# A recurrent chain of RNN, LSTM and mixture of experts: the RNN begins on the first 16 steps of x, and the LSTM follows 8 steps behind it

## The reference

```
x = x + rnn(x, cond)     # h = tanh(h @ Wh + x_t @ Wx + b), 256 steps, h0 = cond
x = x + lstm(x, cond)    # i, f, o, g from x_t @ Wx + b + h @ Wh; c = f*c + i*g; h = o*tanh(c)
x = x + moe(x, cond)     # shared expert gelu(x@sw1+sb1)@sw2+sb2, plus the 2 best of 4 experts,
                         # chosen per batch row from means of x over time
x = x + adapter(x, cond) # low-rank weights made from cond: gelu(x @ (down + a2 b2)) @ (up + a1 b1)
```

## Time and profile before

| | us |
|---|---|
| median of 3 runs | 1098.54 (1098.54 to 1099.82) |
| the profiled execution | 1100.26, its span 1098.3 |
| first RNN tanh | 19.06 |
| first LSTM gate activation (block 0 begins) | 39.60 |
| block 0 | 41.73 |
| block 8 (with low-rank rows), block 10 (plain) | 40.19, 38.68 |
| block 15 begins | 638.08 |

### The profile page before, as it was taken

The page is one execution under the profiler, slowest core; times in us unless marked ns, Lnnn a source line. Parts: engine busy times, 40 slices in busy tenths (PEclk is TensorE's granted clock), DMA queues, the critical chain, the costliest instruction groups (busy, mean ns, idle before and its releaser), DMA issues. The chain is left out here.

```text
span 1098.3 us, 56330 instructions
## 1 busy us (share of the span) xinstructions
PE 1068.6 (97%) x22334; PEld 979.2 (89%) x22334; DVE 825.8 (75%) x3566; ACT 649.0 (59%) x2495; POOL 287.0 (26%) x864
## 2 busy tenths in 40 slices
PE   6899999999999999999999999899999999999998
PEld 5789999899999999999999987788888888888887
DVE  6677878778877878887887786876666666676797
ACT  4567777677777777777777755333333333343476
POOL 3533333333333333333333310560000000000041
PEclk8759999999999999999999998999999999999999
DMA  8401211211211200000000011100000000000022
GB/s 262 104 23 57 62 28 57 62 43 42 61 50 36 64 22 19 19 19 19 19 9 5 4 33 14 17 1 2 2 1 2 2 2 2 2 4 2 3 92 82
DMA packets 54921, 37.01 MB, mean 34 GB/s; under 512 B 25560, under 2 KB 53514, under 8 KB 54668
## 3 DMA queue, kind: packets, MB, share of 16 engines
q1 hardware_dynamic: 54060, 33.12, 10.8%
q10 hardware_dynamic: 608, 0.30, 0.1%
HBM read 28.42 MB, written 4.98 MB: 30 GB/s over the span
## 5 line engine op out<-in xcount | busy, mean ns | idle before, releaser
L657 ACT ACTIVATE gel<-bank,seq 128x256 f32<-128x256 f32 x256 | 121.5, 475 | 215.2 <-PE bank L1298 211.3
L1296 PE MATMUL bank<-XHL,WE 128*128 128x256 f16 x768 | 210.3, 274 | 1.9 <-DVE XHL L883 1.3
L1296 PE MATMUL bank<-GH,WE 128*128 128x256 f16 x768 | 209.4, 273 | 2.5 <-DVE GH L910 1.8
L1298 PE MATMUL bank<-XHL,WE 128*128 128x256 f16 x768 | 210.7, 274 | 0.0
L1297 PE MATMUL bank<-XHL,WE 128*128 128x256 f16 x768 | 210.6, 274 | 0.0
L1298 PE MATMUL bank<-GH,WE 128*128 128x256 f16 x768 | 209.5, 273 | 0.0
L1297 PE MATMUL bank<-GH,WE 128*128 128x256 f16 x768 | 209.5, 273 | 0.0
L448 POOL TENSOR_TENSOR RH<-rf,RH 128x32 f16<-128x32 f32 x256 | 75.6, 295 | 395.4 <-ACT RH L597 395.3
L1296 PE MATMUL bank<-seq 128*128 128x64 f16 (+2 forms) x1216 | 165.4, 203 | 1.9 <-DVE oz L945 1.4
L1298 PE MATMUL bank<-seq 128*128 128x64 f16 (+2 forms) x1216 | 165.8, 204 | 0.0
L1297 PE MATMUL bank<-seq 128*128 128x64 f16 (+2 forms) x1216 | 165.8, 204 | 0.0
(11 more groups left out here) (218 smaller groups left out, 3362.6 us busy)
## 6 DMA issues: line engine op xcount, KB each, us to landing
stage<-in_L_cond_ew SPq DMA_DIRECT2D x64, 128.0 KB, 2.4
stage<-in_L_cond_W SPq DMA_DIRECT2D x32, 256.0 KB, 3.7
XHL<-in_x SPq DMA_DIRECT2D x8, 512.0 KB, 9.1
out<-WE SPq DMA_DIRECT2D x16, 256.0 KB, 2.2
stage<-in_L_cond_sw SPq DMA_DIRECT2D x2, 1024.0 KB, 5.4
scratch<-rows SPq DMA_DIRECT2D x96, 8.0 KB, 1.9
stage<-in_L_cond_Wx SPq DMA_DIRECT2D x1, 1024.0 KB, 9.2
stage<-in_L_cond_Wh SPq DMA_DIRECT2D x1, 1024.0 KB, 11.4
```

What stands on the lines that cost most here:

```text
L657: nc.scalar.activation(gel[:, m % 2, :], banks[m % len(banks)][:, 0:256], ACT.Gelu_apprx_tanh, scale=scale, bias=bias).then_inc(s["a_g"], 1)
L1296: MM(out_, w(HI), x(HI), start=start, stop=False, skip_group_check=True)
L1298: return MM(out_, w(HI), x(LO), start=False, stop=stop, skip_group_check=True)
```

## The change

1. **First x.** The first 16 times of all batches are loaded by 16 DMAs of 16 KB, 8 on SyncE's queue and 8 on ScalarE's ahead of its other loads; eight transposes in two banks turn them, ScalarE and VectorE copy one tile each. The RNN starts on that. The rest of x (8 DMAs of 512 KB) is loaded after the LSTM's weights, into a part of WE that the experts' weights fill later.
2. **Lag.** The LSTM runs LAG = 8 steps behind the RNN: 8 RNN steps alone in place of 16, with two LSTM weight pieces after each. TensorE has two x tiles after each of the lone steps 5, 6 and 7 and two before block 0. Block 15 gets 8 RNN steps.
3. **Turning the rest of x.** All 16 tiles are turned in block 0, in two banks (5 and 6) in place of four. TensorE turns tiles 0 and 1 ahead of LSTM step 0, tiles 2u+2 and 2u+3 at the end of steps u = 0, 1, 2, and tiles 8 to 15 one by one at the ends of steps 7 to 14. A tile waits for the copy of the tile two before it. ScalarE copies the even ones, VectorE the odd ones, at the ends of the steps in `X_OUT`.
4. **Tables.** New `HALVES`, `HALVES_LOW`, `X_TILES`, `EXPERT`, `EXPERT_LOW`, `SHARED_PIECES` (steps 3 to 15 in place of 0 to 14); the next block's x parts are made in steps 4 to 7 of the block before it; GpSimd splits x at other steps of a group; one seed moves by a step; two pieces of the gate's work in block 15 move by one or two steps.

```diff
-PAIR_FROM = 1
+LAG = 8
-        x_bank = [bank[0:4], [*bank[5:8], bank[1]]]
+        x_bank, cond_bank = bank[5:7], bank[7]
...
+        def load_first(engine, batches):
+            for b in batches:
+                engine.dma_start(xin_first[U * (b % G):U * (b % G) + U, b // G, :], a["x"][b, 0:U, :]
+                                 ).then_inc(s["ld_xf"], 16)
...
             # SyncE
-                for quarter in range(4):
-                    load_x(0, quarter)
+                load_first(sp, range(G))
                 ... RNN weights, biases, LSTM weights
-                for quarter in range(4):
-                    load_x(1, quarter)
+                for half in range(2):
+                    for quarter in range(4):
+                        load_x(half, quarter)
...
             # ScalarE
             act.sem_inc(s["a_g"], M)
+                load_first(act, range(G, B))
...
+            def x_out(k):
+                act.wait_ge(s["pe_x"], k + 1)
+                dst, src = x_tile(k)
+                nc.scalar.activation(dst, src, ACT.Copy).then_inc(s["a_x"], 1)
...
-            for r in range(U):
-                rnn_step(0, r)
+            for n in range(LAG):
+                rnn_step(n)
+                for _ in range(LSTM_PIECES[n]):
...
-                    if not last:
-                        rnn_step(it + 1, u)
+                    if it * U + u + LAG < T:
+                        rnn_step(it * U + u + LAG)
...
+                    for k in X_OUT[u] if first else ():
+                        if k % 2 == 0:
+                            x_out(k)
...
             # TensorE
+            def transpose_x(k):
+                half, i = divmod(k, 8)
                 if i % C == 0:
                     pe.wait_ge(s[f"ld_x{half * 4 + i // C}"], 16)
+                if k < 2:
+                    pe.wait_ge(s["v_xf" if k % 2 else "a_xf"], 1)
+                else:
+                    pe.wait_ge(s["v_x" if k % 2 else "a_x"], k // 2)
+                for j in range(4):
+                    last = nc.tensor.transpose(x_bank[k % 2][:, j * P:(j + 1) * P],
+                                               xin[:, half, 4 * (i // C) + j, (i % C) * P:(i % C + 1) * P], idf[:])
                 last.then_inc(s["pe_x"], 1)
...
+            for n in range(LAG):
+                rnn_step(n)
+                if n == LAG - 3:
+                    pe.wait_ge(s["v_wlo"], N_RNN + N_LSTM // 2)
+                    pe.wait_ge(s["v_const"], 6)
+                    ig_x(0, 0)
+                    ig_x(0, 1)
+                elif n == LAG - 2:
+                    ig_x(0, 2)
+                    ig_x(0, 3)
+                elif n == LAG - 1:
+                    f_x(0, 0, 0)
+                    f_x(0, 1, 0)
             for i in range(C):
                 o_x(0, i, 0)
+            for k in X_OUT[0]:
+                transpose_x(k)
             pe.wait_ge(s["v_wlo"], LSTM_SPLIT)
-            pe.wait_ge(s["v_x"], 12)
...
                     next_x(it * U + u)
+                    if first and u + 1 < U:
+                        for k in X_OUT[u + 1]:
+                            transpose_x(k)
...
-HALVES = [0, 2, 3, 2, 2, 3, 2, 2, 0, 2, 3, 2, 2, 3, 2, 2]
-HALVES_LOW = [0, 2, 3, 2, 3, 3, 2, 3, 0, 2, 3, 2, 1, 1, 2, 3]
+HALVES = [0, 3, 2, 1, 3, 2, 2, 3, 0, 3, 2, 1, 3, 2, 2, 3]
+HALVES_LOW = [0, 3, 2, 1, 3, 2, 2, 3, 1, 3, 3, 1, 2, 1, 2, 3]
-LSTM_PIECES = [0, 0, 2, 2] + [1] * 12
-X_HI, X_LO = (10, 14), (11, 15)
+LSTM_PIECES = [2] * LAG
+X_HI, X_LO = (4, 6), (5, 7)
+X_OUT = [(2 * u, 2 * u + 1) if u < 4 else (u,) if u >= 8 else () for u in range(U)]
-X_TILES = [[("f", 0)], [("f", 1), ("o", 0), ("o", 1)], [("ig", 0)], [("ig", 1), ("ig", 2), ("ig", 3)],
-           [("f", 0), ("f", 1)], [("o", 0)], [("o", 1), ("ig", 0), ("ig", 1)], [("ig", 2), ("ig", 3)]]
-EXPERT, EXPERT_LOW = (1, 5, 8, 13), (1, 6, 9, 12, 14)
+X_TILES = [[], [], [("f", 0), ("f", 1), ("o", 0)], [("ig", 0), ("ig", 1), ("ig", 2), ("ig", 3), ("o", 1)],
+           [], [("ig", 0), ("o", 0), ("o", 1)], [("f", 0), ("f", 1), ("ig", 1)], [("ig", 2), ("ig", 3)]]
+EXPERT, EXPERT_LOW = (1, 11, 13, 15), (1, 9, 12, 14, 15)
-SHARED_PIECES = [(u,) for u in range(U - 2)] + [(U - 2, U - 1), ()]
+SHARED_PIECES = [(), (), (), (0,), (1,), (2, 3), (4,), (5,), (6,), (7,), (8, 9), (10,), (11, 12), (13,), (14,), (15,)]
```

More of the change, by code:

```diff
@@ L450, in rnn_step @@
                 nc.gpsimd.tensor_tensor(x, x, rf[:, slot], ALU.add).then_inc(s["p_x1"], 1)
[L451 to L460, removed]
+                if n % H == H - 1:
+                    split_x1(n // H, HI)
+                if n >= H and n % H == 0:
+                    split_x1(n // H - 1, LO)
             def split_x1(k, part_):
@@ L488, in _ @@
             nc.gpsimd.memset(gate_bias[:, NIG + C:NIG + 2 * C], 0.0).then_inc(s["p_gate_bias"], 1)
[L489 to L493, removed]
+            for n in range(LAG, T):
+                rnn_step(n)
+            split_x1(T // H - 1, LO)
             pool.wait_ge(s["v_oh"], 1)
@@ L1061, in block_steps @@
                 for u in range(U):
-                    lstm_step(it, u, not last)
+                    lstm_step(it, u, it * U + u + LAG < T)
                     if last and u in extras:
                         extras[u]()
-                    x_at = X_LO_LOW if low_block(it) else X_LO
-                    if it < NB - 2 and u in x_at:
-                        x_lo(it + 2, x_at.index(u))
+                    if it < NB - 1 and u in X_LO:
+                        x_lo(it + 1, X_LO.index(u))
+                    for k in X_OUT[u] if first else ():
+                        if k % 2:
+                            x_out(k)
                     if u in QUARTERS:
@@ L1330, in _ @@
             for c in range(C):
-                last = nc.tensor.transpose(bank[4][:, (C + c) * B:(C + c + 1) * B], ln[:, c * P:(c + 1) * P],
+                last = nc.tensor.transpose(cond_bank[:, (C + c) * B:(C + c + 1) * B], ln[:, c * P:(c + 1) * P],
                                            idf[0:B, 0:B])
@@ L1337, in _ @@
                 for c in range(C):
-                    last = MM(bank[4][:, 64 + m * B:64 + (m + 1) * B], AW1[:, c, m * P:(m + 1) * P], lnT[:, c, :],
+                    last = MM(cond_bank[:, 64 + m * B:64 + (m + 1) * B], AW1[:, c, m * P:(m + 1) * P], lnT[:, c, :],
                               start=(m == 0 and c == 0), stop=(c == C - 1), skip_group_check=True)
@@ L1598, in block_steps @@
                     lstm_step(it, u)
-                    if not last:
-                        rnn_step(it + 1, u)
-                    elif u == 7:
+                    if it * U + u + LAG < T:
+                        rnn_step(it * U + u + LAG)
+                    elif u == 9:
                         modulation()
-                    elif u == 12:
+                    elif u == 13:
                         logits()
```

166 lines of the change are left out of this document (73 added, 93 removed).

## The result

| | before | after |
|---|---|---|
| median (range) of 5 runs, us | 1098.54 (1097.62 to 1099.82) | 1104.09 (1102.42 to 1106.36) |
| the profiled execution, its span | 1100.26, 1098.3 | 1103.3, 1101.5 |
| ratio of times | | 1.0051, 95% interval 1.0035 to 1.0067 |

The change makes the kernel slower by 0.51%. The forecast was 1100, no change within 0.2%, at 0.31. Slower had 0.36, by rivals C, D and E. The time lies inside the range of 1093 to 1106, which is 13 us wide and was made to hold all the rivals.

What follows compares the result with a forecast made beforehand. TensorE's work was taken to bound blocks 8 and 10, the recurrence and half clock blocks 0 and 15. The terms summed to +1.6 us on 1100.26, so 1101.9 profiled, about 1100 as median; range 1093 to 1106.

Steps and rivals of the forecast that it cites:

- Rival C: Block 0 and the gap before it: the two banks' wait with half clock throughout makes the kernel slower, 1104; chance 0.21.
- Rival D: Blocks' tables cost more: late x tiles and waits on the RNN's split, 0.3 a block, 4 us, 1104; chance 0.11.
- rival E: At the start, the small loads cause delay: plus 7 to 8 us in all, 1106; chance 0.04.
- start, to the first tanh: Start: TensorE's RNN projection begins at 13.95 in place of 17.05, after loads and VectorE's 6.6 us of work: minus 3.1 us.
- lone RNN steps: RNN steps before the LSTM: 18.53 us for 15 intervals become 8.1 for the first seven: minus 10.4 us.
- last tanh to first gate: Gap before block 0: four x tiles of the RNN's end and two transposed tiles at half clock: plus 2.4 us.
- steps 0 to 2 of block 0: Transposes waiting for two banks hold up the next LSTM step; steps of 5.4, 4.3, 4.3 us: plus 5.9.
- steps 3 to 15, with the clock: Rest of block 0: eight more transposed tiles and their copies, plus 3.3, less 0.4 for block 1's clock.
- blocks 1 to 14: New tables leave light steps at the recurrence's floor: plain blocks lose 0.48, low-rank ones 0.2, together plus 4.5 us.
- block 15, first to last gate: Last block: 8 RNN steps add 0.3, step 1 no longer at half clock saves 0.9: minus 0.6 us.
- Rival A: Block 0: dense transposes lift the clock, so steps 0 to 2 cost 12.5; sum -3.2, 1095; chance 0.20.
- Rival B: Later blocks don't lose, since the new table fits: the 4.5 becomes 0, 1096; chance 0.14.

Runs made afterwards that it cites:

- e1: The changed kernel with the transposes of X_OUT[u] inside step u, behind the RNN's matmuls, not at the end of the step before: 1098.66 us, ratio 1.0003.
- e2: The changed kernel with a third bank (7) for the transposed tiles of x, order unchanged: 1102.59 us, ratio 1.0039.
- e4: The changed kernel with one half moved from step 15 to 8 in plain blocks, one x tile from step 2 to 1 of each eight: 1101.74 us, ratio 1.0027.
- e5: The changed kernel with the old tables and the old place of the F seed, at lag 8: 1307.76 us, ratio 1.1909.
- e9: The changed kernel with the transposes' order of e1, the tables of e4 and the sums of e8, keeping its own start: 1094.46 us, ratio 0.9962.
- e10: The changed kernel, unedited, run beside e9 on the same chip: 1104.36 us, ratio 1.0054.
- e3: The kernel before with only the new HALVES, X_TILES and EXPERT tables and the F seed a step earlier: 1106.79 us, ratio 1.0079.
- e8: The changed kernel with the edits of e1 and e4, first x by one DMA, and VectorE's first block sum moved from step 0 to 10: 1093.86 us, ratio 0.9959.

## Why the prediction was right and where it failed

| term | forecast | measured |
|---|---|---|
| start, to the first tanh | -3.1 | -0.90 |
| lone RNN steps | -10.4 | -9.92 |
| last tanh to first gate | +2.4 | +1.31 |
| steps 0 to 2 of block 0 | +5.9 | +5.40 |
| steps 3 to 15, with the clock | +2.9 | +2.76 |
| blocks 1 to 14 | +4.5 | +6.60 |
| block 15, first to last gate | -0.6 | -0.27 |
| behind the last gate | 0 | -1.78 |
| span | +1.6 | +3.20 |

**The start failed in size, by 2.2 us.** The step was "from 17.05 becomes 13.95". The issues went as priced (0.46 in place of 0.40 each, square root 7.76 in place of 7.3). What failed is the 6.6 us for VectorE behind it: I summed VectorE's own operations and left out who releases them. 0.97 for loads, 0.83 more for the eight matmuls L1347 (1.89; their like before, L1338, took 1.06) and the GELU at the end were not in the sum, and the first projection came at 16.17. The 0.83 is a price of the change itself. TensorE in the kernel before:

```profile
5.24 1.97 PE L1322 MATMUL bank<-idf,XHL 128*128 128x128 f32 x8 [1.84 <-DMA XHL<-in_x]
9.81 1.10 PE L1322 MATMUL bank<-idf,XHL 128*128 128x128 f32 x8 [0.30 <-DMA XHL<-in_x]
13.24 1.06 PE L1338 MATMUL bank<-lnT,WE 128*128 128x16 f32 x8 [0.66 <-DVE lnT L863]
```

Among its 32 transposes of half of x the clock rose to full, and was so from 9.36 to 16.19. The new start has four in their place (the change's description says eight), 1.11 us of work at 6.12, and TensorE stays at half clock until 28.79. And what is left may be spread: seven profiles with the new start (after, e1, e2, e4, e5, e9, e10) have their first tanh at 18.00 to 19.13, mean 18.53, the two with the old one (before, e3) at 19.06 and 18.18, mean 18.62. No gain of the start itself is shown. The small loads landed 1.7 to 1.8 us (median) after their issue and overlapped, so the row's reading as latency held, and rival E fell. The Trainium skill (DMA: Bandwidth & Descriptors, "Anatomy of one DMA — SWDGE (gpsimd) path") puts a fixed 2.0 us on each DMA, most of it completion latency, and it is about DMAs that GpSimd issues, where these come from SyncE and ScalarE. The measured 1.7 to 1.8 are near it; that eight in series would take 16 us was my use of it and not what it says.

**The lone steps** came as worked out. **The gap** was 1.1 less than priced. A tile at half clock was priced at 1.07, which does not follow from 1.09 less a drain of 0.15, and is 0.87 by the pair from 36.72 to 38.45; and the clock rose to full at 28.79, in the middle of the pair, which took 1.26 from start to start (28.05 to 29.31). Rival A's 1.4 for the gap, at full clock, was near the 1.31; the end of 1.0 in the forecast had left out the x tile.

**Steps 0 to 2 held**, mechanism and size: 14.0 forecast, 13.49 measured; but 5.4, 4.3, 4.3 was wrong in its split (4.57, 4.66, 4.26), since step 0's copy ended 3.5 after the LSTM's begin (32.83, 29.31) and not 4.2, and the pair of step 1 stood at half clock (1.94 against 1.06). That these two nearly cancel is luck. e1 and e2 take wait and half clock away and the steps shrink. Rival C (16.3 for them, +5 after) fell: steps 3 to 15 took only 2.76 more. Rival A had part of the truth, since block 0's clock rose from 0.58 to 0.79, but steps 0 to 2 took 13.49 and not its 12.5.

**Blocks 1 to 14 failed in size, by 2.1 us** (2.5 with the 0.4 that I booked to block 1's clock). The step was "A plain block loses 0.48". It loses 0.78 on average (six: 232.29 to 236.94), a low-rank one 0.24 (eight: 324.46 to 326.41; forecast 0.2). I let a step without x tiles (0, 1, 4, 8, 9, 12) fall to TensorE's work of 2.28 or the recurrence's 2.31. In block 10 four of them did; step 1 took 2.52 and step 4 took 2.37. In step 1 the queue of VectorE, late from step 0, sets it, as e8 shows. Step 2 takes 2.56 for work that the prediction's terms put at 2.49; a weight load waits 0.19 there for a GELU of the fills (at 451.56), a cause that is read in the trace and not tested. Steps 1 and 2 make up what block 10 loses beyond the forecast (0.71 in place of 0.48); that the six plain blocks lose 0.78 on average is left open. Light steps expose every delay that full ones hid. Rival D named the right stage and a wrong cause (the split of the RNN's output, 8 steps ahead, holds nobody with the new tables; e5 shows it does with the old). Rival B (no loss) fell by e3.

**Block 15** got the 0.9 that I gave its step 1 (3.40 to 2.52), and lost most of it again in small sums.

**Behind the last gate** the changed kernel is 1.78 faster with the same code, 419.98 against 421.76. The other kernels lie between 420 and 421.8; it stays unexplained and may be spread.

**From the sum to the median.** The terms were 1.6 too small in the span, and that is as small as it is by luck: the start and the blocks missed by 2.2 and 2.1 one way, the gap by 1.1 and the unexplained 1.78 behind the last gate the other. The rest of the miss of 4.1 us is in how a profiled execution stands to the median: I took 1.7 off because the kernel before was profiled that much above its median, and the changed one was profiled 0.8 under its own. Of the 5.5 us between the medians the spans show only 3.2; the medians' interval is 3.8 to 7.4 us.

## What to carry to other kernels

A transpose or copy queued ahead of a recurrence's matmuls costs its own time, and if its bank is still being emptied it costs that wait as well, and here the clock with it: put it behind the short work of the same step, where the bank has come free. When work is taken out of steps that one engine fills, ask first what the other engines do there, since a step falls only to the next late queue. And sum a start along its releasers, not along one engine's operations.

## What was not expected of the hardware

- The same eight transposes of a pair took 1.06 us at 32.98 and 1.94 at 36.72: the granted clock was 1.00 from 28.79 to 35.62 and 0.50 from there to 42.44, and TensorE had stood idle for 1.4 us of each step. In e1, with no such idle stretch, it stayed at 1.00 from 33.68 to 47.33.
- The granted clock of a window is not to be trusted ahead of the trace's first record of it (28.79 in the changed kernel, 33.68 in e1). The windows say 1.00 there, but matmuls of 128 columns began 0.107 us apart at 17 us and 0.055 apart at 31 us.
- In e5 waits of 2.2 us every fourth step went with a granted clock of 0.75 in block 10 and 0.875 in the span (0.987 in the changed kernel), and the kernel lost 83 us beyond the waits.
- 32 transposes of 16 columns took 3.59 us, 0.11 each, about half of the 0.21 from one start to the next of the 128-column ones at half clock (eight in 1.73, 36.72 to 38.45), for an eighth of the columns. A load of 256 KB onto 16 partitions landed after 4.9 us, one onto 128 after 3.0.
- Profiles of kernels with the same start have their first tanh up to 1.1 us apart (18.00 in e9, 19.13 in e4), so a term of 1 us of the start can't be read from one pair of profiles.
- In the kernel before, TensorE did nothing but transposes up to 12.6, and the third group of eight took 1.10 us (at 9.81) where the first two took 1.97 and 1.95: its clock rose to full at 9.36 on transposes alone. The Trainium skill (TensorE: Matmul & The Clock Gate, "Part 4: PE-mode transpose") says that the full clock does not engage for transpose mode. These f32 transposes, shown as MATMUL with an identity, had it; whether they run in that mode, the trace does not say.
